# First attention: the output sums of the pairs of units alternate between two PSUM banks

## The reference

```python
x = x + tanh(g_xattn[0]) * L0_xattn(layernorm(x), ctx)   # 32 heads of 8 values, rotary positions
x = x + tanh(g_ffn[0])   * L0_ffn(layernorm(x))          # mixture of 8 experts, 2 chosen, and a shared one
x = x + tanh(g_xattn[1]) * L1_xattn(layernorm(x), ctx)   # 16 heads of 128 values
x = x + tanh(g_ffn[1])   * L1_ffn(layernorm(x))          # mixture of 8 experts, 2 chosen
```

```python
logits = einsum('bqhd,bkhd->bhqk', q, k) / sqrt(8)
w      = softmax(logits)
attn   = einsum('bhqk,bkhd->bqhd', w, v)
return attn @ Wout + bout
```

## Time and profile before

| | before |
|---|---|
| median of 3 runs | 1811.49 us (1809.84 to 1813.02) |
| the profiled execution | 1808.37 us, of which span 1806.6 us |
| TensorE busy | 1620.6 us, 90% of the span |
| VectorE busy | 1167.7 us, 65% |
| ScalarE busy | 735.4 us, 41% |
| GpSimd busy | 411.5 us, 23% |

### The profile page before, as it was taken

The page is one execution under the profiler, slowest core; times in us unless marked ns, Lnnn a source line. Parts: engine busy times, 40 slices in busy tenths (PEclk is TensorE's granted clock), DMA queues, the critical chain, the costliest instruction groups (busy, mean ns, idle before and its releaser), DMA issues.

```text
span 1806.6 us, 42368 instructions
## 1 busy us (share of the span) xinstructions
PE 1620.6 (90%) x14740; PEld 1362.5 (75%) x14740; DVE 1167.7 (65%) x3031; ACT 735.4 (41%) x1492; POOL 411.5 (23%) x448
## 2 busy tenths in 40 slices
PE   3899999978999899997799999999999997699998
PEld 2566666646777689997688888888888886588887
DVE  5877777785667655555666666666666654465655
ACT  2566666652232225554233333333333332344343
POOL 3555555531313310000112111122122101000000
PEclk9999999989999999999899999999999998799999
DMA  6666666651101014434000000000000000000000
GB/s 175 143 120 120 121 121 120 119 98 51 53 24 36 35 36 142 152 124 164 27 25 21 26 20 25 22 20 24 26 20 26 20 14 4 3 24 12 12 24 24
DMA packets 127356, 107.06 MB, mean 59 GB/s; under 512 B 10442, under 2 KB 120195, under 8 KB 127020
## 3 DMA queue, kind: packets, MB, share of 16 engines
q1 hardware_dynamic: 121068, 89.07, 20.9%
q0 software_dynamic: 6208, 16.95, 2.9%
HBM read 49.22 MB, written 56.77 MB: 59 GB/s over the span
## 4 chain that ended last, share of the span: by engine, by line
PE 54%; DVE 26%; issue 10%; ACT 6%; DMA 2%; DVEq 1%; ACTq 1%; SPq 0%; POOL 0%; POOLq 0%
PE bank L536 11%; PE bank L538 10%; PE bank L537 10%; PE bank L1015 4%; PE bank L607 2%; PE bank L621 2%; PE bank L598 2%; PE bank L1043 2%; DVE probs_b L2269 2%; DVE rm_b L2266 2%; PE bank L562 2%; PE bank L638 2%; DVE x L2170 1%; DVE oT_b_lo L2258 1%; PE bank L625 1%
## 5 line engine op out<-in xcount | busy, mean ns | idle before, releaser
L1575 POOL TENSOR_TENSOR probs_b<-probs_b,rs_b 128x512 f32<-128x512 f32 x64 | 66.8, 1043 | 483.1 <-DVE rs_b L2279 482.8
L1404 ACT ACTIVATE probs_b<-probs_b 128x512 f32<-128x512 f32 x64 | 40.4, 632 | 323.6 <-DVE probs_b L2269 323.6
L536 PE MATMUL bank<-xT_b_hi,m_hi 128*128 128x256 f32 x512 | 153.8, 300 | 20.0 <-ACT qT L1383 12.0
L536 PE MATMUL bank<-n_hi,oT_b_hi 128*128 128x256 f32 x512 | 150.0, 293 | 5.6 <-DVE x L2237 5.6
L537 PE MATMUL bank<-xT_b_hi,m_lo 128*128 128x256 f32 x512 | 145.8, 285 | 0.0
L538 PE MATMUL bank<-xT_b_lo,m_hi 128*128 128x256 f32 x512 | 145.6, 284 | 0.0
L537 PE MATMUL bank<-n_hi,oT_b_lo 128*128 128x256 f32 x512 | 145.3, 284 | 0.0
L538 PE MATMUL bank<-n_lo,oT_b_hi 128*128 128x256 f32 x512 | 145.3, 284 | 0.0
L1015 PEld LDWEIGHTS bank<-ctxT_b,qT 128*128 128x128 f32 x1024 | 126.5, 194 | 2.8
L1187 ACT ACTIVATE probs_a<-probs_a 128x512 f32<-128x512 f32 x128 | 80.3, 627 | 110.7 <-DVE probs_a L1711 110.2
L1015 PE MATMUL bank<-ctxT_b,qT 128*128 128x64 f32 x1024 | 123.0, 274 | 0.0
(11 more groups left out here) (316 smaller groups left out, 4790.9 us busy)
## 6 DMA issues: line engine op xcount, KB each, us to landing
sorted_x<-zeros SPq DMA_DIRECT2D x16, 2112.0 KB, 14.6
xg<-sorted_x SPq DMA_DIRECT2D x71, 128.0 KB, 2.1
sorted_y<-ys SPq DMA_DIRECT2D x71, 128.0 KB, 1.9
w_raw<-in_w SPq DMA_DIRECT2D x16, 408.0 KB, 3.8
x<-in_x SPq DMA_DIRECT2D x4, 1024.0 KB, 7.3
cx_raw<-in_ctx SPq DMA_DIRECT2D x32, 128.0 KB, 2.7
out<-x SPq DMA_DIRECT2D x8, 512.0 KB, 2.9
ctxT_a<-in_ctxT SPq DMA_DIRECT2D x16, 128.0 KB, 2.1
```

Of the source, the lines that this page charges most:

```text
L536: pe.matmul(dst, lh, rh, start=start, stop=False, skip_group_check=True)
L1575: pool.tensor_tensor(probs_b[b], probs_b[b], rs_b[:, b, :].unsqueeze(2).broadcast_to([P, G1, S]), ALU.mult).then_inc(s["b_probs"], 1)
```

## The change

Bank 6, which nothing else uses in these rounds, takes the outputs and sums of pairs 1 and 3; bank 4 keeps those of pairs 0 and 2. The outputs of a pair then wait for `weigh0` of the pair two before, since that one was the last to use the bank. The next round's pair 0 follows pair 3, so the alternation goes on across rounds. `inv_a`, the buffer of the reciprocals, is still a single one. Before, TensorE's wait saw to it that VectorE had finished with `inv_a`; now `weigh0` itself waits until VectorE's last product has been counted.

```diff
+        def out_bank(p):
+            return bank[4 + 2 * (p % 2)]
...
                 if hh == 0:
-                    pe.wait_ge(s["a_oT_ready"], START + i * 4 + p)
+                    pe.wait_ge(s["a_oT_ready"], START + i * 4 + p - 1)
                 for b in range(2):
                     for j in range(4):
-                        m = pe.matmul(bank[4][32 * j:32 * j + 32, 64 * b:64 * b + 64],
+                        m = pe.matmul(out_bank(p)[32 * j:32 * j + 32, 64 * b:64 * b + 64],
...
                 for j in range(4):
-                    m = pe.matmul(bank[4][32 * j:32 * j + 32, P:2 * P], total_a[:, hh, :], pT_a[n % 2][:, j, :],
+                    m = pe.matmul(out_bank(p)[32 * j:32 * j + 32, P:2 * P], total_a[:, hh, :], pT_a[n % 2][:, j, :],
...
             def weigh0(i, p):
 
                 ve.wait_ge(s["a_o_psum"], START + i * NS + 2 * p + 2)
-                st.done(ve.reciprocal(inv_a, bank[4][:, P:2 * P]))
+                ve.wait_ge(s["a_oT_ready"], START + i * 4 + p)
+                st.done(ve.reciprocal(inv_a, out_bank(p)[:, P:2 * P]))
                 ve.wait_ge(s["a_y_psum"], START + i * 2 + p // 2 - 1)
                 st.wait()
-                ve.tensor_tensor(oT_a[:, p, :], bank[4][:, 0:P], inv_a, ALU.mult).then_inc(s["a_oT_ready"], 1)
+                ve.tensor_tensor(oT_a[:, p, :], out_bank(p)[:, 0:P], inv_a, ALU.mult).then_inc(s["a_oT_ready"], 1)
```

## The result

The changed kernel takes 1801.36 us (median of 5 runs, 1797.56 to 1802.47), the kernel before in the same comparison 1810.62 us (5 runs, 1809.84 to 1813.02). The ratio is 0.9944, with a 95% interval of 0.9933 to 0.9954: faster by 9.3 us, where 10.6 were forecast. (The ratio is the recorded one and not the quotient of the two medians, which is 0.9949.) By the bound of 0.2% it is faster.

The account below looks back on a forecast made before the run. A round of the first attention was taken as bound by a circle through TensorE, VectorE and ScalarE, no engine full. 8.8 + 0.8 + 1.0 = 10.6 us, so 1811.49 - 10.6 = 1800.9 us; range 1797 to 1806.5.

Parts of the forecast that it names:

- The outputs of unit 2 start 1.13 us sooner: Each loop round of the first attention: TensorE starts these outputs once the transposes are out, 1.13 us sooner.
- The copy of unit 4 is late next: Each round, TensorE newly waits 0.50 us for ScalarE's copy behind unit 6's exponential; 0.63 us of 1.13 gained.
- second releaser: ScalarE's copy of unit 4, which TensorE's outputs of unit 4 wait for; called 0.63 us behind.
- VectorE's extra row: One more wait row in each of 64 weigh0, hidden behind earlier work: 0 us, at most 2.1 us.
- 14 rounds by 0.63 us, 8.8 us: Loop of the first attention: a round shrinks from 22.585 to 21.95 us, 14 times, 8.8 us.
- The first round, 0.8 us: Idle time of 0.81 us ahead of unit 2's outputs, read as the old wait, goes; bounds 0 and 0.8.
- The last round, 1.0 us: Two TensorE waits of 0.50 us for the product both go: 1.0 us, bounds 0 and 1.0.
- Moved as a whole: Everything after the first attention starts from its end and was taken to shift as a whole.
- The whole wait: Rival, chance 0.04: all 16.8 us of the wait plus the first round's 0.8 are won, 17.6 us, 1793.9 us.
- closed by VectorE alone: Rival of no change, chance 0.07: VectorE alone sets the round and its 1.85 us idle only moves; 1811.5 us.
- the rows cost nothing: Against the slower rival, chance 0.05: extra rows stall VectorE ahead of the reciprocal; at 0.5 us each, 1815.9 us.
- only part is won: Rival, chance 0.11: smaller gain of 6.7 or 4.4 us through lost terms, row cost or a later copy; 1804.8 to 1807.1 us.

Follow-up runs that it names:

- second bank alone: Changed kernel with outputs alternating between two banks, but TensorE's old wait and no extra wait on VectorE: ratio 1.0002, round 22.585 us.
- extra wait alone: Kernel before, one bank and TensorE's old wait, with only VectorE's wait on a_oT_ready added ahead of the reciprocal: ratio 1.0008, round 22.594 us.
- changed, again: The changed kernel run once more without an edit, as control: 1803.04 us against 1810.65, ratio 0.9964.
- more rows: Changed kernel with four more semaphore increments between the wait and the reciprocal of each weigh0: 1801.44 us, ratio 0.9952.
- six kernels with a changed order: Kernels with unit 4's copy, pair 0's weigh0 (one or two banks), next scores, or the last two together (two or one bank) moved earlier: 1785.71 to 1796.22 us.
- pair 0 first: Kernel before, one bank and old wait, with weigh0 of pair 0 moved ahead of the next round's queries on VectorE: 1794.91 us, ratio 0.9904.

## Why the prediction was right

**The outputs of unit 2 start 1.13 us sooner, what stands behind them is free.** Right: no gap ahead of the outputs of unit 2 and unit 3.

**The copy of unit 4 is late next, 0.63 us of 1.13 are won.** Right, and shown by two runs. The round is 21.966 us against 21.95 forecast, the new wait 0.52 us against 0.50, the waits for `pT_a` 16.5 us against about 16, VectorE's idle time 1.21 us against 1.2. Moving the copy gave the rest back (0.59 us a round), and the second bank without the looser wait gave nothing. The prediction calls the second releaser "0.63 us behind"; that is what was left to win, and what it holds back is 0.50 us by its own sum, 0.52 us measured. The rule of the Trainium skill, Perfetto Trace Analysis, section Matmuls, to rotate independent groups through banks so that evacuation and matmuls overlap, is true here for the wait that it removes; the trace shows that the next releaser decides how much of it is kept.

**No cost for VectorE's extra row.** Right: 0.009 us a round with one row on the kernel before, no difference with four more on the changed one. In the Trainium skill, Perfetto Trace Analysis, section Sequencer-only Instruction, such a row holds the sequencer for as long as its wait lasts. No cost of that is seen in the time here: the trace shows the next reciprocal start before the work ahead of it has ended. One figure of the argument was off: VectorE's own product lies 2.7 us ahead of the next reciprocal at the closest (262.49 to 265.23 us before), not at least 3 us; the wait for it is over all the same.

**14 rounds by 0.63 us, 8.8 us.** Right in size: 13 rounds measured give 285.56 us against 293.60, 8.04 us, and one more at 0.62 makes 8.7 us.

**The first round, 0.8 us.** This is the term that failed. TensorE's timeline after the change, from 34 to 80 us, against the earlier trace rows:

```profile
56.58 0.43 PE L624 MATMUL bank<-pT_a,v_bd 128*32 128x64 f32 x16
...
61.15 1.09 PE L601 MATMUL bank<-k_hd,q_rot 32*64 32x256 f32 x16
...
75.93 0.27 PE L628 MATMUL bank<-pT_a,total_a 128*32 128x128 f32 x1 [1.02 <-issue]
```

The wait ahead of the outputs of unit 2 is gone, as I had read it, and between these two executions the stretch from the first largest of pair 0 to the next round's scores is 0.85 us shorter (62.92 - 36.48 = 26.44 us and 61.15 - 35.56 = 25.59 us). But up to the second half of the queries of round 2 only 0.35 us of it are left (41.62 and 41.27 us), and in the profiles of the experiments nothing is. With the old waits that distance is 41.62, 41.89 (second bank alone) and 41.97 us (extra wait alone), in the mean 41.83; with the new waits it is 41.27, 42.02 (changed, again) and 42.20 us (more rows), in the mean 41.83 as well. The wait itself depends on the execution. From the scores of pair 3 to the next round's scores, for the kernel before:

```profile
55.87:62.92 7.05, 6.24 (x119) 4.15 (x119) 6.81 (x12) 5.36 (x13) 6.27 (x7) 1.00 0.34 76
```

and for the one with the extra wait alone, followed by the row with its wait:

```profile
57.06:64.91 7.85, 7.60 (x119) 5.00 (x119) 6.62 (x12) 5.48 (x13) 6.28 (x7) 0.78 0.34 75
...
59.55 0.66 PE L621 MATMUL bank<-pT_a,v_bd 128*32 128x64 f32 x16 [0.24 <-DVE oT_a L1721]
```

At a granted clock of 1.00 (2.4 GHz) TensorE waits 0.81 us there. At 0.78, a mean over time at both levels (1.2 and 2.4 GHz), it comes to the outputs later itself, and waits 0.24 us, or not at all (second bank alone). The clock was 1.00 in the first profile of either kernel, where TensorE had idled 1.42 and 2.15 us ahead of the scores of pair 3, and 0.78 in the four others, where it had idled 2.47 to 2.64 us; at 0.78 the stretch takes 7.68 and 7.85 us with the old waits, 7.66 and 7.69 us with the new. The prediction read the 0.8 us from the one execution it had. Its lower bound of 0, put there for the gap that no wait explains, was the better value.

**The last round, 1.0 us.** Right, a little more. From the queries of round 15 to the memset it was 415.32 - 371.70 = 43.62 us and is 403.01 - 362.39 = 40.62 us: 3.0 us, of which 0.62 belong to round 15. The rest is divided by the scores of pair 3 of the last round, before and after:

```profile
401.13 1.09 PE L598 MATMUL bank<-k_hd,q_rot 32*64 32x256 f32 x16
```

```profile
389.95 1.09 PE L601 MATMUL bank<-k_hd,q_rot 32*64 32x256 f32 x16
```

From there to the memset it was 14.19 us and is 13.06 us. These 1.13 us go with the two waits of 0.50 us each, and they repeat: 14.19 to 14.20 us in all five profiles with the old wait of TensorE, whatever the order, 13.05 to 13.07 us in all seven with the new one. The remaining 1.25 us lie ahead of these scores and go with TensorE's granted clock. In the last round TensorE stands idle for 6.65 us ahead of the scores of pair 2, for the centring of pair 1, and the granted clock is low after it. In about equal distances from there, before:

```profile
393.00:398.00 5.00, 3.49 (x40) 2.13 (x44) 4.67 (x11) 2.06 (x4) 0.00 (x0) 0.50 0.00 0
398.00:402.00 4.00, 4.00 (x61) 2.25 (x50) 2.86 (x6) 2.87 (x8) 0.00 (x0) 0.70 0.00 0
```

After:

```profile
383.00:388.00 5.00, 3.42 (x44) 2.01 (x44) 4.67 (x11) 1.99 (x4) 0.00 (x0) 0.53 0.00 0
388.00:392.00 4.00, 4.00 (x86) 2.40 (x74) 3.90 (x8) 3.06 (x9) 0.00 (x0) 1.00 0.00 0
```

In the second stretch the clock was 0.70 and 61 matmuls fitted in, then 1.00 and 86. With the changed kernel again it is 0.79 at this place (388.86 to 392.86 us), and from the scores of pair 2 to those of pair 3 the six executions took 6.62, 5.33 and 5.38 us with the old waits, 5.37, 6.27 and 6.03 us with the new. So when the clock comes back differs between executions, and the 1.25 us are scatter.

**Moved as a whole.** The stage gained 9.8 us by the means of three profiles each: (378.8 + 377.8 + 378.1) / 3 = 378.2 us for those with the old round, (367.4 + 368.9 + 369.0) / 3 = 368.4 us for those with the new. That is about 8.8 us for 14 rounds, about 1 us for the last and nothing for the first; the 0.8 us that the forecast has too many are the first round's. The whole gained 9.3 us in the first comparison and 7.6 and 9.2 us in the second. The rest behind the memset is 1391.3, 1396.7 and 1393.0 us with the old round, and 1397.7, 1398.6 and 1395.0 us with the new one. The mean is 3.4 us apart, but the two groups overlap, and the kernels with still shorter rounds, which start the later stages earlier still, have 1394.1 to 1397.3 us. So the 6.4 us between the first two profiles are mostly the scatter of two executions, the one before being the shortest of all twelve. The six kernels with a changed order don't show a loss either: their medians lie 16.5 to 27.1 us below the kernel before, 22.3 us in the mean, and their stages are 17.0 to 27.2 us shorter than 378.2 us, 21.2 us in the mean. Whether a loss of 1 us or so belongs to the change remains open; no experiment was made that would hold the start of the later stages fixed.

**The rivals.** The whole wait was not won (waits for `pT_a` grew), the round was not closed by VectorE alone (its idle time fell by 0.64 us and didn't turn up elsewhere), and the rows cost nothing. That only part is won (4.4 to 6.7 us) is out for the stage, which gained 9.8 us. For the whole, the first comparison leaves it out (0.9933 to 0.9954 is 8.3 to 12.1 us), the second doesn't by itself (0.9952 to 0.9976 is 4.3 to 8.7 us).

What the prediction did not see is that the bank was not needed. It read correctly that the product came late, and took the order that makes it late as given. VectorE idled 2.68 us ahead of the queries, and in the timeline with pair 0 first its outputs are there after 0.91 us of that, with 0.96 + 0.29 = 1.25 us of work to do.

## What to carry to other kernels

When a wait for a buffer is to be removed, look for the releaser that comes second and how much later it is: here 0.5 of 1.13 us went to it in each round. Before spending a second buffer, try whether the producer of the wait, or the one that is late next, can move into its engine's own idle time, and whether work for which another engine idles can be issued ahead of the group that waits: with one bank, two such moves gained 1.8 us a round where the second bank gained 0.6. Behind these moves the second bank is worth nothing in a round of the loop and 1.1 us in the last one. A wait that is read from one execution, in a stretch that is passed once, is worth checking in a second: the first round's 0.8 us stood in one profile and not in the others. Stop when the engine behind it is full, since the moves don't add beyond that.

## What was unexpected of the hardware

- The same stages with the same instructions took 1391.3 to 1398.6 us in twelve profiled executions, more than half of what the whole change gained; a round repeated to 0.02 us. For a gain of this size the round is the surer measure.
- After TensorE's idle time of 6.65 us in the last round the same work took 5.33 to 6.62 us in the six executions compared, by when the granted clock came back. In the first round the clock was 1.00 in two executions and 0.78 in four, and with the old waits the lower clock left 0.24 us or nothing of a wait of 0.81 us.
- Up to five rows with waits and counts ahead of a reciprocal cost nothing behind 0.6 us of work.
- In the first pass through the loop there is a gap of 0.86 us (before) or 1.02 us (after) that no wait explains, 0.44 us with the changed kernel again. It isn't in later rounds.
